# Five rotating buffers for expert weights, and weight splits moved away from the 128-row tiles, in a decoder layer on one core

## The reference, cut to what matters

```
h = x @ w1[i] + b1[i]            # 256 -> 2048
a, g = split(h, 2)               # 1024 each
y = (a * sigmoid(g)) @ w2[i] + b2[i]   # 1024 -> 256
out = out + where(top1 == i, y, 0)
```

## Time and profile before

| | us |
|---|---|
| median of three runs | 1238.18 (1238.03 to 1238.29) |
| the profiled execution's own time | 1236.09 |
| its span, first to last instruction | 1234.4 |
| PE busy in the span | 1098.6 (89%) |
| DVE busy | 838.1 (68%) |
| ACT busy | 587.0 (48%) |
| POOL busy | 620.3 (50%) |

### The profile page before, as it was taken

The page is one execution under the profiler, slowest core; times in us unless marked ns, Lnnn a source line. Parts: engine busy times, 40 slices in busy tenths (PEclk is TensorE's granted clock), DMA queues, the critical chain, the costliest instruction groups (busy, mean ns, idle before and its releaser), DMA issues. The chain is left out here.

```text
span 1234.4 us, 21275 instructions
## 1 busy us (share of the span) xinstructions
PE 1098.6 (89%) x7718; PEld 915.0 (74%) x7718; DVE 838.1 (68%) x1517; ACT 587.0 (48%) x1000; POOL 620.3 (50%) x526
## 2 busy tenths in 40 slices
PE   4999689999998999999999999708999989899998
PEld 2655457777777778687778888607998979789887
DVE  4699347778648876568784554355888778676785
ACT  1254423545515545334455444315676656555663
POOL 6349107666538585477575122322555354453542
PEclk9999899999999999999999999958999999998999
DMA  8533301111220111201112111155576666665670
GB/s 189 147 123 124 96 20 45 47 30 47 38 62 19 37 33 36 54 12 44 33 38 46 38 39 39 22 191 173 203 242 229 213 231 214 235 229 201 230 268 29
DMA packets 94020, 134.09 MB, mean 109 GB/s; under 512 B 40929, under 2 KB 75444, under 8 KB 88029
## 3 DMA queue, kind: packets, MB, share of 16 engines
q1 hardware_dynamic: 78813, 111.68, 28.9%
q0 software_dynamic: 15104, 21.06, 6.2%
HBM read 111.50 MB, written 23.91 MB: 110 GB/s over the span
## 5 line engine op out<-in xcount | busy, mean ns | idle before, releaser
L1787 DVE TENSOR_TENSOR wlow<-staged,whigh 128x2048 fp32r<-128x2048 f32 x69 | 159.1, 2306 | 6.1 <-ACT whigh L1884 6.1
L1997 PE MATMUL psH<-xhigh,whigh 128*128 128x256 f32 x512 | 146.5, 286 | 11.4 <-DVE glow L1818 8.4
L1884 ACT ACTIVATE whigh<-staged 128x2048 fp32r<-128x2048 f32 x69 | 132.4, 1919 | 50.1 <-DMA staged<-in_L_ffn_w 50.1
L1666 POOL TENSOR_TENSOR idle<-e_less 128x1 f32<-128x1 f32 x42 | 49.8, 1186 | 195.8 <-DMA ids_now<-ids 101.5
L1997 PE MATMUL psH<-xlow,whigh 128*128 128x256 f32 x512 | 144.0, 281 | 0.0
L1997 PE MATMUL psH<-xhigh,wlow 128*128 128x256 f32 x512 | 144.0, 281 | 0.0
L1394 PEld LDWEIGHTS psD<-vo,pT 128*128 128x128 f32 x1024 | 124.8, 193 | 24.2 <-issue 20.5
L1394 PE MATMUL psD<-vo,pT 128*128 128x128 f32 x1024 | 135.0, 279 | 6.9 <-issue 5.2
L748 ACT ACTIVATE pT<-psA 77x512 f32<-77x512 f32 x128 | 75.8, 593 | 71.5 <-PE psA L1376 68.9
L1997 PEld LDWEIGHTS psH<-xhigh,whigh 128*128 128x128 f32 x512 | 98.6, 193 | 13.4 <-DVE gated L1804 9.1
L704 ACT ACTIVATE o2T<-psA 128x512 f32<-128x512 f32 x64 | 38.2, 597 | 141.8 <-PE psA L1404 141.2
(11 more groups left out here) (268 smaller groups left out, 2876.5 us busy)
## 6 DMA issues: line engine op xcount, KB each, us to landing
staged<-in_L_ffn_w SPq DMA_DIRECT2D x69, 1024.0 KB, 5.1
tokens<-out_rows POOLq DMA_DIRECT2D x32, 256.0 KB, 6.3
kT<-k_cols SPq DMA_DIRECT2D x16, 308.0 KB, 2.9
vo<-v_rows SPq DMA_DIRECT2D x16, 308.0 KB
xb<-in_x SPq DMA_DIRECT2D x32, 128.0 KB
b2s<-in_L_ffn_b SPq DMA_DIRECT2D x23, 128.0 KB
k_cols<-qT SPq DMA_DIRECT2D x4, 616.0 KB
v_rows<-pT SPq DMA_DIRECT2D x4, 616.0 KB
```

Of the source, the lines that this page charges most:

```text
L1666: nc.gpsimd.tensor_tensor(idle[:, i:i + 1], e_less_8[:, 0:1], e_less_8[:, 0:1], ALU.add)
L1787: tt(wlow[par][:, i, :], staged[:, i, :], whigh[par][:, i, :].bitcast(F32), ALU.subtract)\
L1884: nc.scalar.activation(whigh[par][:, i, :], staged[:, i, :], ACT.Copy).then_inc(w_high[i], 1)
L1997: ins = mm(psH[:, q % 2 * PAIR + c, part, :], lhs, rhs, start=i == 0, stop=i == len(passes) - 1)
```

## The change

The pieces of weights no longer have a buffer each: they pass through five buffers in turn (the two new ones in `staged_more`), piece n of the whole row of 69 pieces going to buffer n modulo 5. `w_high` and `w_split`, three counters each before, become one counter each, and a load waits for the split of the piece five before it.

The splits are put elsewhere in the lists. Next to a big tile nothing changes for pieces 1 and 2. A small tile does none in its steps 2 and 3: its next tile's piece 1 is split at the end of the tile before, behind `finish`, and piece 2 in the step 0 of the next tile. Piece 0 is split ahead of `finish(t)` instead of behind it, for all tiles. ACT's copies move along. Last, the wait for gate_low of two steps before goes from `hidden` of a small tile to its `turn_gated`.

```diff
+W_BUFFERS = 5
+        staged_more = sb("staged_more", [P, W_BUFFERS - 3, HC * C])
-        w_high = [sem(f"w_high{i}") for i in range(PIECES)]
-        w_split = [sem(f"w_split{i}") for i in range(PIECES)]
+        w_high, w_split = sem("w_high"), sem("w_split")
+        def piece(t, i):
+            n = t * PIECES + i
+            k = n % W_BUFFERS
+            return n, k, staged[:, k, :] if k < 3 else staged_more[:, k - 3, :]
 # SP, load_piece
-                if wait:
-                    sp.wait_ge(w_split[i], t)
+                n, k, rows = piece(t, i)
+                if n >= W_BUFFERS:
+                    sp.wait_ge(w_split, n - W_BUFFERS + 1)
 # SP, before the tiles
-            load_piece(2, expert(2), 0)
+            third = expert(2)
+            for i in range(PIECES):
+                load_piece(2, third, i)
 # SP, tile
-                if exists(t + 2):
-                    e = expert(t + 2)
-                    load_piece(t + 2, e, 1)
-                    load_piece(t + 2, e, KC)
+                if exists(t + 3):
+                    e = expert(t + 3)
+                    load_piece(t + 3, e, 0)
+                    load_piece(t + 3, e, 1)
                 sp.wait_ge(y_done, t + 2)
                 if exists(t + 2):
-                    load_bias(t + 2, e)
+                    load_bias(t + 2, expert(t + 2))
                 if exists(t + 3):
-                    load_piece(t + 3, expert(t + 3), 0)
+                    load_piece(t + 3, e, KC)
 # DVE, tile
                     late_low(t, q)
-                    if exists(t + 1):
-                        low_part(t + 1, 1 - par, q - 1)
+                    if IS_BIG[t] and exists(t + 1):
+                        low_part(t + 1, q - 1)
                     early_low(t, q)
...
                     early_low(t + 1, 0)
+                    if not IS_BIG[t]:
+                        low_part(t + 1, KC)
                     gate(t + 1, 1)
                     late_low(t + 1, 1)
+                    if exists(t + 2):
+                        low_part(t + 2, 0)
...
                 finish(t, slot)
-                if exists(t + 2):
-                    low_part(t + 2, par, 0)
                 if exists(t + 1):
+                    if exists(t + 2) and not IS_BIG[t + 1]:
+                        low_part(t + 2, 1)
                     early_low(t + 1, 1)
 # ACT, tile
                 late_high(t, 2)
-                if exists(t + 1):
-                    high_part(t + 1, 1 - par, 2)
+                if IS_BIG[t] and exists(t + 1):
+                    high_part(t + 1, KC)
...
                     if exists(t + 2):
                         high_tokens(t + 2, par)
-                        high_part(t + 2, par, 0)
-                    early_high(t + 1, 0)
+                    if not IS_BIG[t]:
+                        early_high(t + 1, 0)
+                        high_part(t + 1, KC)
+                    if exists(t + 2):
+                        high_part(t + 2, 0)
+                    if IS_BIG[t]:
+                        early_high(t + 1, 0)
 # PE, hidden
-                if item >= 2 and not IS_BIG[(item - 2) // PAIRS_HID]:
-                    pe.wait_ge(g_split, item - 1)
                 if IS_BIG[t]:
+                    if item >= 2 and not IS_BIG[(item - 2) // PAIRS_HID]:
+                        pe.wait_ge(g_split, item - 1)
 # PE, turn_gated
-                pe.wait_ge(h_done, t * PAIRS_HID + q + 3)
+                item = t * PAIRS_HID + q
+                pe.wait_ge(h_done, item + 3)
+                if not IS_BIG[(item - 2) // PAIRS_HID]:
+                    pe.wait_ge(g_split, item - 1)
```

More of the change, by code:

```diff
@@ L134, in decoder_layer @@
         scattered = [whole.enter_context(nc.semaphore(f"scattered{i}")) for i in range(2)]
-        w_in = [whole.enter_context(nc.semaphore(f"w_in{i}")) for i in range(3)]
+        w_in = [whole.enter_context(nc.semaphore(f"w_in{i}")) for i in range(W_BUFFERS)]
         tables = unit_rows, slot_no, slot_row, region_row
@@ L1593, in expert, with load_piece @@
                 return sp.value_load(tile_ei[0:1, slot:slot + 1], min_val=0, max_val=E - 1)
-            def load_piece(t, e, i, wait=True):
-                if wait:
-                    sp.wait_ge(w_split[i], t)
+            def load_piece(t, e, i):
+                n, k, rows = piece(t, i)
+                if n >= W_BUFFERS:
+                    sp.wait_ge(w_split, n - W_BUFFERS + 1)
                 if i < KC:
                     src = w1[bass.ds(e, 1), i * P:(i + 1) * P, :].rearrange("a p n -> p (a n)")
-                    sp.dma_start(staged[:, i, :], src).then_inc(w_in[i], 16)
+                    sp.dma_start(rows, src).then_inc(w_in[k], 16)
                 else:
                     src = w2[bass.ds(e, 1)].rearrange("a (k p) n -> p (a k) n", p=P)
-                    sp.dma_start(staged[:, i, :].rearrange("p (k n) -> p k n", k=HC), src).then_inc(w_in[i], 16)
+                    sp.dma_start(rows.rearrange("p (k n) -> p k n", k=HC), src).then_inc(w_in[k], 16)
             def load_bias(t, e):
@@ L1628, in _ @@
             for i in range(PIECES):
-                load_piece(0, first, i, wait=False)
+                load_piece(0, first, i)
             sp.wait_ge(located, 2)
@@ L1782, in _, with low_part @@
             nc.vector.memset(seed[:, 1:2], 0.0).then_inc(h_done, 2)
[L1784 to L1788, removed]
+            def low_part(t, i):
+                n, _, rows = piece(t, i)
+                dve.wait_ge(w_high, n + 1)
+                tt(wlow[t % 2][:, i, :], rows, whigh[t % 2][:, i, :].bitcast(F32), ALU.subtract).then_inc(w_split, 1)
             def low_tokens(t, par):
@@ L1858, in tile @@
                 finish(t, slot)
-                if exists(t + 2):
-                    low_part(t + 2, par, 0)
                 if exists(t + 1):
+                    if exists(t + 2) and not IS_BIG[t + 1]:
+                        low_part(t + 2, 1)
                     early_low(t + 1, 1)
             locate()
-            low_part(0, 0, 0)
-            low_part(0, 0, 1)
+            low_part(0, 0)
+            low_part(0, 1)
             low_tokens(0, 0)
@@ L1869, in _ @@
             gate(0, 0)
-            low_part(0, 0, 2)
+            low_part(0, 2)
             gate_low(0, 0)
@@ L1873, in _ @@
             gate(0, 1)
-            low_part(1, 1, 0)
+            low_part(1, 0)
             gate_low(0, 1)
@@ L1880, in _, with high_part @@
         def _(act):
-            def high_part(t, par, i):
-                act.wait_ge(w_in[i], 16 * (t + 1))
-                nc.scalar.activation(whigh[par][:, i, :], staged[:, i, :], ACT.Copy).then_inc(w_high[i], 1)
+            def high_part(t, i):
+                n, k, rows = piece(t, i)
+                act.wait_ge(w_in[k], 16 * (n // W_BUFFERS + 1))
+                nc.scalar.activation(whigh[t % 2][:, i, :], rows, ACT.Copy).then_inc(w_high, 1)
             def high_tokens(t, par):
@@ L1943, in tile @@
                     if exists(t + 2):
-                        high_part(t + 2, par, 1)
+                        high_part(t + 2, 1)
                     early_high(t + 1, 1)
@@ L1949, in _ @@
             for i in range(KC):
-                high_part(0, 0, i)
+                high_part(0, i)
             high_tokens(0, 0)
-            high_part(0, 0, KC)
+            high_part(0, KC)
             act.wait_ge(h_done, 2)
@@ L1956, in _ @@
             gate_high(0, 0)
-            high_part(1, 1, 0)
+            high_part(1, 0)
             sigmoids(0, 1)
             gate_high(0, 1)
-            high_part(1, 1, 1)
+            high_part(1, 1)
             tiles(tile)
@@ L1982, in hidden @@
                     pe.wait_ge(x_split, t + 1)
-                    pe.wait_ge(w_split[0], t + 1)
-                    pe.wait_ge(w_split[1], t + 1)
+                    pe.wait_ge(w_split, piece(t, 1)[0] + 1)
                     if not IS_BIG[t]:
@@ L2023, in down @@
                 if q == 0:
-                    pe.wait_ge(w_split[KC], t + 1)
+                    pe.wait_ge(w_split, piece(t, KC)[0] + 1)
                     pe.wait_ge(y_done, t + 1)
```

## The result

The change makes the kernel slower: 1261.55 us (1260.6 to 1263.92, four runs) against 1238.11 beside it, a ratio of 1.0205 with a 95% interval of 1.017 to 1.024. The forecast had the sign, but its range ended at 1249. The profiled execution took 1260.60 us, 24.5 more than the one of before; 3.2 had been forecast.

What follows compares the result with a forecast made beforehand. PE was taken as the bound, busy 369.35 of 392.40 us in the experts' stretch. Terms -16.6 + 6.3 + 10.9 + 2.6 = +3.2 us on 1238.18 gave 1241.4 us, range 1233.5 to 1249.

Steps and rivals of the forecast that it cites:

- The six waits of 1.33: `hidden` of a big tile behind a small one, as in tile 19: six waits of 1.33 us, forecast to stay.
- the walk: The prediction's instruction-by-instruction timing through tiles such as 17, 18 and 19, from which it sized the waits.
- +6.3: Nine big tiles behind big ones: `down` waits 0.70 us more each because `finish` stands behind a split; 6.3 us added.
- +10.9: Six big tiles behind small ones: `down` waits 1.81 us each, with two ACT copies in a row; 10.9 us added.
- POOL's loop: From POOL's add behind one `finish` to the next `finish`: 16.0 us after the change, late by 0.4 in two tiles, taken as nothing.
- the 0.76 of the prediction: In POOL's loop, the time before its add behind `finish`, raising the loop from 16.8 to 17.6 us.
- the second rival: POOL's loop stays the bound, `finish` late in small tiles 6, 9, 12, 15: 4 us taken, 1245.4 us; chance 0.13.
- the sign of being wrong: `finish` waiting for POOL, one of the signs listed as showing the forecast wrong; no size given.
- cost nothing but by their place: Loads, copies, splits and SP register loads: same number as before, so no cost except by place.
- The clock: PE's clock falls behind one in four of the six 1.81 us waits, 1.7 us per fall; 2.6 us added.
- the first (clock): Rival: the clock falls behind most of the new 1.81 waits; all six give +10.8, 1249.0 us; chance 0.13.
- The third, a quicker pace of PE: Rival: new waits put up to half of 2,472 matmuls on a quicker pace; -5.0, 1233.2 us; chance 0.24.

Runs made afterwards that it cites:

- e7: The changed kernel with SP's `w2` load moved behind the wait for the scatter and the load of row numbers: 1243.67 us against 1236.72 for the kernel before, ratio 1.0068.

## Why the prediction was wrong, point by point

**What held.** In the group of big tiles behind big ones six of nine waits are 0.55 to 0.59, which with the 0.16 of the units is 0.7 to 0.76, as walked. The six waits of 1.33 stay, `hidden` of a small tile no longer waits, and POOL's add is under 1 us. In tile 19 ACT does the walk's steps, ghigh, two copies in a row, and the sigmoid:

```profile
1190.43 0.63 ACT L1924 ACTIVATE ghigh<-gated 128x512 fp32r<-128x512 f32 x1 [0.40 <-DVE gated L1814]
1190.96 1.90 ACT L1899 ACTIVATE whigh<-staged_more 128x2048 fp32r<-128x2048 f32 x1
1192.77 1.90 ACT L1899 ACTIVATE whigh<-staged 128x2048 fp32r<-128x2048 f32 x1
1194.57 0.81 ACT L1915 ACTIVATE sig<-psH,b1s 128x256 f32<-128x256 f32 x2
```

In e7 the six waits behind small tiles are 1.51 to 1.65; 1.81 less 0.16 had been forecast. So the +6.3 and the +10.9 were right for what they priced. The sign was not luck either: in e7, without POOL's loop, the change still costs time.

**The step that failed is the one on POOL's loop**, "loop 16.0, late by 0.4 in two tiles, taken as nothing". The loop takes 1071.95 - 1053.98 = 17.97 from one `finish` to the next. The 1.6 of the shorter add were there and were lost again behind it. From `finish` to the second add it is 12.50 instead of 13.04 (1103.00 less 1089.96, the 0.76 of the prediction taken off the 1090.72 in the earlier trace rows): only 0.54 of the 1.6 come through (0.42 against the same tile of the kernel before), because the scatter lands with the load beside it and not sooner for being issued sooner. In the kernel before it landed behind a load too; the walk had let the landing follow the issue. From there to `finish` it is 5.47 instead of 4.52, because the gather's second issue takes 2.00 next to the split that now stands there. Five `finish` waited for the bias, 1.21, 0.67, 2.27, 2.28 and 2.27, 8.7 us in all, where the second rival had 8 at most and took 4. `finish` waiting for POOL was also the sign of being wrong that the prediction had named.

The loads "cost nothing but by their place", said the prediction, and put that place at nothing. It had a price: e7 moves one load alone and takes 17.9 us away.

**A term that was missing: a split that POOL stretches.** The walk took every split at 2.28. In four tiles where POOL's bias or gather runs beside the split it took more, and the wait of `down` grew by as much:

```profile
938.81 4.03 DVE L1798 TENSOR_TENSOR wlow<-staged_more,whigh 128x2048 fp32r<-128x2048 f32 x1
942.76 0.68 DVE L1849 TENSOR_TENSOR ys<-psY,xs 128x512 f32<-128x512 f32 x1
```

In tile 5 that is 1.75 more and the wait is 2.33 = 0.58 + 1.75. Likewise 0.62 in tile 3 (wait 1.20), 1.19 in tile 18 (1.59) and 0.51 in tile 19 (2.11). With 0.15 in tile 7 it is 4.2 us. The prediction had used the exclusion of the two engines ("SBUF — State Buffer", Who interferes with whom, in the Trainium skill) in one direction alone, for POOL's add. It works in the other too: in tile 18 the bias of 1.29 lies wholly inside the split and lengthens it by 1.19.

A wait of 1.59 in tile 2, 1.0 above the walk, has the same cause in another instruction: while POOL's bias ran, gate_low took 2.52 us instead of 0.68, and the gate and the split behind it came late.

```profile
881.33 2.52 DVE L1825 TENSOR_TENSOR glow<-gated,ghigh 128x512 fp32r<-128x512 f32 x1 [1.33 <-ACT ghigh L1924]
881.99 1.31 POOL L1694 TENSOR_TENSOR xs<-xs,b2s 128x512 f32<-128x512 f32 x1
```

So of the 32.4 - 18.2 = 14.2 us that the waits are longer than walked, 8.7 are `finish` waiting for POOL, 4.2 stretched splits and 1.0 this one.

**The clock** was priced at 2.6 for the waits of 1.81, one fall in four. Behind those six waits it fell twice (in tiles 10 and 19, behind 1.86 and 2.11), 3.4 us by the 1.7 each. That was about right. The other four falls follow waits of 2.33 to 2.81 in tiles 5, 9, 12 and 15, which the walk did not have. That is 6.8 us, again from POOL, by its loop or by a stretched split. In sum the six cost 20.4 / 2 = 10.2, 7.6 more than taken.

The account closes: 3.2 forecast, 14.2 more of waits and 7.6 more of clock make 25.0 us; 24.5 were measured, for the profiled executions. Of the rivals, the first (clock) and the second (POOL) both came, and not each alone: four of the six falls stand behind waits that POOL made. The third, a quicker pace of PE, had no part that shows: at the full clock matmuls that follow each other without a wait start 0.116 us apart on average, before and after.

**What stays open.** Why the shifted loads are worth 6.8 us with `finish` first and nothing with the split first. And what drops the clock: in the changed kernel it fell behind waits of 1.86 (tile 10) and 2.11, not behind another of 1.86 in tile 16 nor behind one of 2.50 in tile 7, and in e7 once, behind 2.04, not behind six of 1.5 to 1.65.

## What to carry to other kernels

A loop over several engines that ends just in time before a change is a bound with zero slack: walk it event by event, with the landing of its transfers, before a saving inside it is counted. Here a 1 MB load issued beside a small scatter that others wait for held the scatter until just behind its own end; where a trace shows that, issue the load behind. And where two engines exclude each other, as POOL's adds and DVE's splits do here, stretch the instructions of both.

## What the runs showed of the hardware

An indirect scatter of two issues, over at 4.4 to 5.1 us behind the end of a big tile's `finish`, landed 7.9 to 9.4 behind that end in the changed kernel, in eleven of fourteen tiles 0.3 to 0.7 after the 1 MB load beside it. In e7, without that load, it landed 5.9 to 8.1 behind the end of `finish`, in ten of the fourteen within 1.5 of the end of its issue. In the kernel before, with a load of `w1` beside it and an issue that was over only at 5.9 to 6.7, it landed at 8.0 to 9.9. The rows of all scatters, from issue to landing, in the changed kernel, e7 and the kernel before:

```profile
DMA to landing us min/median/max: 2.1/4.5/7.2
```

```profile
DMA to landing us min/median/max: 2.1/3.2/5.4
```

```profile
DMA to landing us min/median/max: 2.1/5.1/7.1
```

The Trainium skill ("DMA: Bandwidth & Descriptors", Issuing engines are not separate DMA queues) says that transfers of SP and POOL interleave on the same engines; the trace agrees, and shows the price.

A POOL issue of an indirect DMA was also longer while DVE ran a split, 1.95 to 2.29 us for the gather's second issue in tiles 9, 12, 15 and 19, against 1.02 in e7's tile 12. The scatter's second issue was too: in the changed kernel 2.25 to 2.90 us where a split ran beside it, 0.97 to 1.00 where none did.
